# Moving the norm, split and transposes of seven graphs out of the start of a graph-attention kernel and into its steps, with 1/sqrt on GpSimd

## What is computed

```python
h = jnp.maximum(_layernorm(x, axis=-1), 0.0)
q, k, v = h @ Wq + bq, h @ Wk + bk, h @ Wv + bv          # 8 heads of 64
scores = einsum('bmhd,bnhd->bhmn', q, k) / 8 + edge_bias[edges]
scores = leaky_relu(scores, 0.2)
scores = where(edges > 0, scores, -1e9)
out = einsum('bhmn,bnhd->bmhd', softmax(scores), v) @ Wp + bp
return x + out
```

## Time and profile before

| what | us |
|---|---|
| median of 3 runs | 1028.54 (1027.62 to 1029.74) |
| the profiled execution | 1028.09 |
| its span in the profile | 1026.3 |
| PE busy | 972.7 (95%) |
| DVE busy | 885.7 (86%) |
| ACT busy | 774.3 (75%) |
| POOL busy | 489.6 (48%) |
| mean granted clock of TensorE | 0.986 |

### The profile page before, as it was taken

The page is one execution under the profiler, slowest core; times in us unless marked ns, Lnnn a source line. Parts: engine busy times, 40 slices in busy tenths (PEclk is TensorE's granted clock), DMA queues, the critical chain, the costliest instruction groups (busy, mean ns, idle before and its releaser), DMA issues. The chain is left out here.

```text
span 1026.3 us, 28211 instructions
## 1 busy us (share of the span) xinstructions
PE 972.7 (95%) x8688; PEld 941.7 (92%) x8688; DVE 885.7 (86%) x3283; ACT 774.3 (75%) x1737; POOL 489.6 (48%) x864
## 2 busy tenths in 40 slices
PE   5578999999999999999999999999999999999995
PEld 4468999999999999999999999999999999999994
DVE  4868899888998989888998899888998889988973
ACT  3577878788778887888787877787787777878852
POOL 1003445455545554555455545554554555545553
PEclk9988999999999999999999999999999999999997
DMA  7573455455555464545455455544555454544431
GB/s 175 185 246 104 128 154 141 137 136 145 138 139 146 124 168 135 144 125 159 123 150 140 134 150 144 145 133 140 150 137 144 120 151 135 162 116 130 104 75 29
DMA packets 226599, 142.21 MB, mean 139 GB/s; under 512 B 35393, under 2 KB 216141, under 8 KB 226445
## 3 DMA queue, kind: packets, MB, share of 16 engines
q1 hardware_dynamic: 225652, 139.80, 49.7%
q10 hardware_dynamic: 792, 0.53, 0.3%
HBM read 79.19 MB, written 44.04 MB: 120 GB/s over the span
## 5 line engine op out<-in xcount | busy, mean ns | idle before, releaser
L1061 POOL TENSOR_SCALAR a_line<-w,a_bias 128x256 f32<-128x256 f32 x512 | 264.8, 517 | 445.2 <-DVE w L1714 401.7
L1249 PE MATMUL bank<-pt,nat_sb 128*65 128x128 f32 x2048 | 266.0, 273 | 0.3
L1691 DVE CUSTOM_DVE_ANT_0 w<-bank,mask_rows 128x256 f32<-128x256 f32 x512 | 196.0, 420 | 78.2 <-issue 65.7
L1249 PEld LDWEIGHTS bank<-pt,nat_sb 128*65 128x65 f32 x2048 | 231.1, 138 | 0.8 <-issue 0.8
L1714 DVE SCALAR_TENSOR_TENSOR w<-w,shift,a_line 128x256 f32<-128x256 f32 x512 | 229.2, 487 | 1.7 <-POOL a_line L1061 1.5
L1474 ACT ACTIVATE pt<-bank 128x512 f32<-128x512 f32 x256 | 154.3, 603 | 101.1 <-PE bank L1202 93.4
L1703 DVE TENSOR_TENSOR onehot<-val,counts_to 128x512 fp32r<-128x512 f32 x256 | 178.1, 696 | 2.2
L1456 ACT ACTIVATE mask_own<-bank,mask_bias 128x512 bf16<-128x512 f32 x256 | 177.0, 691 | 1.1 <-PE bank L1226 1.1
L1465 ACT ACTIVATE t_sb<-bank 128x512 fp32r<-128x512 f32 x256 | 152.3, 595 | 4.0 <-PE bank L1214 3.9
L1202 PE MATMUL bank<-ident,w 128*128 128x128 f32 x1024 | 154.3, 273 | 0.0
L1191 PE MATMUL bank<-t_sb,q_hi 128*128 128x256 f32 x512 | 143.4, 302 | 3.5 <-DVE wmax L1691 3.0
(11 more groups left out here) (136 smaller groups left out, 1604.0 us busy)
## 6 DMA issues: line engine op xcount, KB each, us to landing
adj_in<-in_adj_dram SPq DMA_DIRECT2D x64, 512.0 KB, 4.0
mask_store<-mask_own SPq DMA_DIRECT2D x64, 512.0 KB, 3.5
mask_rows<-mask_store SPq DMA_DIRECT2D x512, 64.0 KB, 2.4
o_pairs<-o_turned SPq DMA_DIRECT2D x128, 128.0 KB
nl_store<-nl_ring SPq DMA_DIRECT2D x7, 512.0 KB, 4.2
stack_store<-stage SPq DMA_DIRECT2D x7, 512.0 KB, 2.9
h_stack<-stack_store SPq DMA_DIRECT2D x7, 512.0 KB, 5.5
h_nl<-nl_store SPq DMA_DIRECT2D x28, 128.0 KB, 3.8
```

The lines of the kernel that those rows point to most:

```text
L1061: nc.gpsimd.tensor_scalar(a_line[:, i % 2, :], w[:, i, :], 5.0, a_bias[:, i:i + 1], ALU.mult, ALU.add)\
L1249: last = pe.matmul(o_part[0:D + 1, P * u:P * u + P], nat_sb[:, t % 2, p % 4 * 2 + u, k, :], pt[:, p % 2, u, k, :], start=(k == 0), stop=(k ...
L1691: nc.vector.tensor_tensor_reduce(w[:, i, :], row_bank[:, SLOTS * u:SLOTS * u + SLOTS], mask_rows[:, t % 2, p % 4 * 2 + u, :], 0.25, LEAST_ ...
```

## The change

Only graph 0 is now prepared at the start. Graph g + 1 is loaded (256 KB of `x`), normed, split and turned in steps of graph g, at lags of its own: X_LOAD 8, CENTER 19, SQUARES 20, VARIANCE 21, RSTD 22, NORMED 25, HIGH 26, LOW 27, TURN_H 30 and 34. `h_nl` and `h_stack` have two slots, one for even and one for odd graphs. Stores of `h` in natural order and both loads are gone; a store of the turned `h` stays (only another branch reads it, which these inputs don't take). 1/sqrt of these graphs is made by POOL with 13 small instructions on 128 x 8 values, each waiting for the one before it (`inverse_roots`); graph 0 keeps ACT's sqrt. The transposes go through `misc`, four at a time. Beta moves from lags 6 and 10 to 10 and 14, the mean vector from 22 to 26.

The folding of the weights is cut in two. `fold_scores` has 16 products in place of 40 (bk is a 65th column of Wk, and bq is multiplied once and copied to both halves), and `fold_values` stands ahead of step 9. ACT does an Exp on one column right after the sqrt, so that its table is loaded there. The three subtractions on `kind_bias` go to the branch not taken.

```diff
-    PARTS = ((0, 8), (8, 32), (32, 64))
 
     LOAD, CONV, COUNT, TURN_A, USED, RANK, VAL, ONEHOT = 0, 4, 6, 5, 7, 8, 9, 9
-    MASK, MASK_OUT, MASK_IN, TFILL, QFILL, BETA, COLSUM, VEC = 10, 14, 15, 13, 9, 6, 18, 22
+    MASK, MASK_OUT, MASK_IN, TFILL, QFILL, BETA, COLSUM, VEC = 10, 14, 15, 13, 9, 10, 18, 26
     SCORE, A_LINE, Y, TURN, PV, X_ADD, MOVE_O, PROJ, NORM, SUM, OUT = 17, 19, 20, 21, 22, 24, 26, 31, 32, 34, 35
-    K0, SETTLED = 32, 24
+    K0 = 32
+
+    X_LOAD, CENTER, SQUARES, VARIANCE, RSTD, NORMED, HIGH, LOW, TURN_H, STORE_H = 8, 19, 20, 21, 22, 25, 26, 27, 30, 35
...
+        def coming(b, s, lag):
+
+            g = every(b, s, lag, PPG)
+            return b + g + 1 if g is not None and b + g + 1 < B else None
...
+            def load_rows(g):
+                if g >= 2:
+                    sp.wait_ge(nl_lo, g - 1)
+                sp.dma_start(rows_of(g), x_tiles[:, tiles_of(g), :]).then_inc(x_in[g % 2], 16)
...
-                g = every(b, s, LOAD, PPG)
-                if g is not None and later(b + g):
-                    if later(b + g, 2):
-                        sp.wait_ge(q_lo_ready, 32 * (b + g) - 31)
-                    load_stack(b + g)
+                g = coming(b, s, X_LOAD)
+                if g is not None:
+                    load_rows(g)
...
-                last = piece(b, s, TFILL + 1, 4)
-                if last is not None and last[0] == TPG - 1 and not (isinstance(b, int) and b == B - 1):
-                    sp.wait_ge(t_filled, 4 * TPG * b + 4 * TPG - 3 + last[1])
-                    if last[1] == 0:
-                        sp.wait_ge(col_sums, b + 1)
-                    load_natural(b + 1, last[1])
+                g = coming(b, s, STORE_H)
+                if g is not None:
+                    store_stack(g)
...
             load_rows(0)
+            load_adj(0, 0)
             sp.dma_start(bp_row, bp.rearrange("(a d) -> a d", a=1)).then_inc(wp_landed, 16)
             sp.dma_start(temp[0:1, 2896:2904], edge_bias[1:2, :]).then_inc(wp_landed, 16)
-            load_rows(1)
-            for t in range(2):
-                load_adj(0, t)
-            load_rows(2)
-            sp.dma_start(kind_bias[:, :, :].rearrange("p k h -> p (k h)"),
-                         edge_bias.rearrange("(a k) h -> a (k h)", a=1).to_broadcast([P, 5 * H])).then_inc(kinds_landed, 16)
+            load_adj(0, 1)
             for half in range(2):
                 load_x(0, half)
-            store_graph(0)
-
             for s in range(K0):
-                if s == MASK_OUT:
-                    sp.wait_ge(square_sums, B)
-                if s == SETTLED:
-                    settle(sp)
                 step(0, s)
-                k = ramp_chunk(s - 1)
-                if k is not None and k < B:
-                    store_graph(k)
...
+            def inverse_roots(g):
+
+                var, root, part = row_var[:, tiles_of(g)], row_rstd[:, tiles_of(g)], newton[:, g % 2]
+                pool.wait_ge(var_ready, g + 1)
+                nc.gpsimd.tensor_scalar(root.bitcast(I32), var.bitcast(I32), -0.5, 1597463007.0, ALU.mult, ALU.add)\
+                    .then_inc(newton_steps, 1)
+                n = 13 * (g - 1) + 1
+                for i in range(3):
+                    pool.wait_ge(newton_steps, n)
+                    nc.gpsimd.tensor_tensor(part, root, root, ALU.mult).then_inc(newton_steps, 1)
+                    pool.wait_ge(newton_steps, n + 1)
+                    nc.gpsimd.tensor_tensor(part, part, var, ALU.mult).then_inc(newton_steps, 1)
+                    pool.wait_ge(newton_steps, n + 2)
+                    nc.gpsimd.tensor_scalar(part, part, -0.5, 1.5, ALU.mult, ALU.add).then_inc(newton_steps, 1)
+                    pool.wait_ge(newton_steps, n + 3)
+                    nc.gpsimd.tensor_tensor(root, root, part, ALU.mult).then_inc(newton_steps, 1)
+                    n += 4
+                pool.wait_ge(newton_steps, n)
+                pool.nop(nofuse=True).then_inc(rstd_ready, 1)
+
             def step(b, s):
                 p = pair(b, s, A_LINE)
                 if p is not None:
                     for u in range(2):
                         line(b, p, u)
+                g = coming(b, s, RSTD)
+                if g is not None:
+                    inverse_roots(g)
...
+            def fold_scores():
+
+                for a, rows in enumerate(both):
+                    for c in range(PAIRS):
+                        pe.matmul(fold_banks[a][0:D, (D + 1) * c:(D + 1) * c + D + 1], wqT[rows, c, :], wkT[rows, c, :],
+                                  start=True, stop=True)
+                        last = pe.matmul(fold_banks[a][0:D, 264 + c:265 + c], wkT[rows, c, 0:D], bq_col[rows, c:c + 1],
+                                         start=True, stop=True)
+                last.then_inc(fold_ready, 1)
+
+            def fold_values():
+
+                pe.wait_ge(wp_landed, 16 * 3)
+                pe.wait_ge(ones_ready, 1)
+                pe.wait_ge(bias_products, PAIRS)
+                for a, rows in enumerate(both):
+                    for c in range(PAIRS):
+                        pe.matmul(value_banks[a][0:D, D * c:D * c + D], wvT[rows, c, :], wp_in[rows, c, :], start=True, stop=True)
+                    sums = value_banks[a][:, 328:332]
+                    pe.matmul(sums, ones[rows, :], bqk[rows, :], start=True, stop=False)
+                    pe.matmul(sums, ones[0:1, :], eb_row[:, a, :], start=False, stop=True)
                 for c in range(PAIRS):
-                    pe.matmul(first[0:D, D * c:D * c + D], wqT[rows, c, :], wkT[rows, c, :], start=True, stop=True)
-                    pe.matmul(first[0:D, 256 + c:257 + c], wqT[rows, c, :], bk_col[rows, c:c + 1], start=True, stop=True)
-                    pe.matmul(second[0:D, D * c:D * c + D], wvT[rows, c, :], wp_in[rows, c, :], start=True, stop=True)
-                    for dst in both:
-                        pe.matmul(second[dst, 256 + c:257 + c], wkT[rows, c, :], bq_col[rows, c:c + 1],
-                                  start=True, stop=True)
-                sums = (o_bank, misc)[a][:, 0:PAIRS]
-                pe.matmul(sums, ones[rows, :], bqk[rows, :], start=True, stop=False)
-                last = pe.matmul(sums, ones[0:1, :], eb_row[:, a, :], start=False, stop=True)
-            last.then_inc(fold_ready, 1)
-            for c in range(PAIRS):
-                pe.matmul(turn_banks[0][:, 0:D], ones, wp_bv[:, c, :], start=(c == 0), stop=False)
-            pe.matmul(turn_banks[0][:, 0:D], ones[0:1, :], bp_row, start=False, stop=True).then_inc(fold_ready, 1)
-            pe.wait_ge(folded, 6)
-
-            def turn_graph(g):
-                pe.wait_ge(nl_lo, g + 1)
-                for j in range(2 * g, 2 * g + 2):
-                    if j >= 2:
-                        pe.wait_ge(stack_copied, j - 1)
-                    for i in range(MT):
-                        last = pe.transpose(halves4[j % 2][:, P * i:P * i + P],
-                                            natural_of(g)[:, MT * (j % 2) + i, :].bitcast(F32), ident[:, :])
-                    last.then_inc(nl_turned, 1)
-
-            turn_graph(0)
-            pe.wait_ge(stack_copied, 2)
-            pe.wait_ge(consts_done, 1)
+                    pe.matmul(value_banks[0][:, 256:256 + D], ones, wp_bv[:, c, :], start=(c == 0), stop=False)
+                pe.matmul(value_banks[0][:, 256:256 + D], ones[0:1, :], bp_row, start=False, stop=True).then_inc(fold_ready, 1)
+
+            def turn_rows(g, j, dst):
+                for i in range(MT):
+                    last = pe.transpose(dst[:, P * i:P * i + P], natural_of(g)[:, MT * j + i, :].bitcast(F32), ident[:, :])
+                last.then_inc(nl_turned, 1)
...
+                        pe.wait_ge(nl_lo, g + 1)
+                        free(q_bank_uses, b, s, i)
+                        turn_rows(g, j, misc)
+                        i += 1
...
-            for s in range(K0):
+            fold_scores()
+            pe.wait_ge(plain_ready, 1)
+            for s in range(COUNT + 1):
                 step(0, s)
-                k = ramp_chunk(s)
-                if k is not None and k < B:
-                    turn_graph(k)
+            pe.wait_ge(nl_lo, 1)
+            for j in range(2):
+                turn_rows(0, j, (t_bank, m_bank)[j])
+            pe.wait_ge(consts_ready, 7)
+            for s in range(COUNT + 1, QFILL):
+                step(0, s)
+            fold_values()
+            pe.wait_ge(folded, 6)
+            pe.wait_ge(stack_copied, 2)
+            for s in range(QFILL, K0):
+                if s == SCORE:
+                    pe.wait_ge(folded, 8)
+                    pe.wait_ge(hi_weights, 10)
+                step(0, s)
...
+            def copy_turned(g, j, src):
+                act.wait_ge(nl_turned, 2 * g + j + 1)
+                if g >= 2 and j == 0:
+                    act.wait_ge(q_filled, 16 * (g - 1))
```

(68 more changed lines are left out.)

235 lines of the change are left out of this document (113 added, 122 removed).

## The result

The changed kernel takes **1038.62 us** (median of 4 runs, 1037.36 to 1039.55), the kernel before, on the same chip, 1028.08 (1026.57 to 1029.74): a ratio of 1.0101, 95% interval 1.0082 to 1.0121. It is 1.0% slower; the prediction was 1018 with a range of 1008 to 1029. The profiled execution has a span of 1036.7 us against 1026.3.

What follows compares the result with a forecast made beforehand. PE was taken to bound full load, a chain of waits the start. Span 1026.3 - 26.0 (start) + 6.1 (PE) + 1 (DVE) + 8.4 (POOL) = 1015.8, so 1018 us measured; range 1008 to 1029.

Steps and rivals of the forecast that it cites:

- The start: Before the first scores: shorter prologue and folding let DVE take them at 48.1, 26.0 us earlier, bounds 20 and 29.
- the working: Chain of waits at the start: query fill at 29.7, 16 us to scores at 45.7; weights landing 1 us sooner.
- the masks: Spread masks at the start: last copy at 38.4, then 10.7 us of store and spreading; scores taken 49.1, less 1.
- PE and DVE at full load: Each graph's added work: eight PE transposes at 0.88 us, 6.1 in seven graphs; DVE 1 us in all, bounds 0 and 4.
- POOL's term: 13 POOL instructions in step 22 delay step 24's lines; PE stalls 1.4 us, six times: 8.4 us, bounds 0 and 28.
- N: Time of POOL's 13 instructions in step 22: 3.5 us at 0.20 + 0.07 each, between 2.9 and 5.5.
- the collisions with DVE: Steps 22 and 23, POOL and DVE holding each other up: 0 to 1.4 us more, 0.2 taken.
- slack: Delay of POOL's lines before step 24 that PE's second projection does not feel: 2.2 us a graph.
- rival 3: POOL's 13 instructions cost near a 128x64 addition (5.5 us) and lose the lock; stall 4.7 us six times, 1038; chance 0.13.
- point of decision: Stall size from which POOL's roots make the kernel slower: 3.1 us (N = 5.3), giving 1028.5.

Runs made afterwards that it cites:

- the seed alone: The changed kernel with no Newton round, 1 POOL instruction in step 22 in place of 13, a root off by per cents: 1010.93 us, ratio 0.9838.
- the filled stall: The changed kernel with 22 useless PE products added in step 24, ahead of the second projection's waits: 1029.06 us, ratio 1.0025.

## Why the prediction was wrong

**The start: right in size, in part by luck.** Forecast: 26.0 us earlier, bounds 20 and 29; measured 24.6. The query fill came at 29.44 (29.7, or 28.7 with the weights 1 us sooner; they were 0.3 sooner). From there to PE's first scores it was 19.2 us and not 16: they came at 48.67, where the working has 45.7 less 1. This didn't show in the total, because the working had the masks as the last to come, at 48.1; they were there earlier, and DVE waited 0.63 us for PE.

**PE and DVE at full load: right.** Forecast 0.88 + 0.14 us a graph, so periods of 118.3; with the seed alone they are 118.3, and PE is busy 0.85 us more a period.

**POOL's term is the step that failed.** The sum has 8.4 us for the 13 instructions, six stalls of 1.4 us. They cost 4.65 us a period, 27.9 in six (122.95 with them, 118.3 with the seed alone): 19.5 us more than the sum has, which is nearly all of the miss of 20.6. It has two halves.

*The stall: the right place, the right engine, the right user, a size too small by half.* Forecast: N = 3.7, the stall N - 2.23 = 1.4 us. Measured: 4.91 and 2.99, which is 9.5 us in six. The term's parts: 13 x 0.28 = 3.6 (forecast 3.5); the collisions with DVE 1.1 (forecast 0.2); 0.24 before the heads, where the semaphore of the last instruction is waited for (0.07 in the forecast); and a slack of 1.9, not 2.2. The largest of them is the choice of 0.2 out of a range of 0 to 1.4: the argument beside it named the one-hots, and each 0.68 us one-hot that runs while small instructions stream can catch one, as two did here and two in the kernel before with the same 13. By the rule of the Trainium skill's "SBUF — State Buffer", section "SBUF: two separate sides", the prediction had the chain sit out 2.0 us. The trace agrees as to the lock: all four that were caught end 0.06 us after DVE's instruction. But each pays only what is left of that instruction when it starts: 0.44, 0.43, 0.09 and 0.12 us.

*The clock: a term that the sum has at nothing, without a reason.* It gave every microsecond of stall one microsecond. With the stall, PE's granted clock fell, and this cost 1.65 us a graph more, as the filled stall shows; 9.9 us in six. By the medians of the two kernels it is 1038.6 - 1029.1 = 9.5, or 7.5 when each is taken against the kernel before of its own group of runs. Without this fall, as the filled kernel shows, the changed one comes out 0.25% above the time before.

**The rivals.** The time of rival 3 (the roots turn the sign; 1038 us) came out, but only half of its mechanism. It wanted instructions near the cost of the 128x64 addition and a stall of 4.7 us; they cost 0.20 us each as forecast, the stall was 3.0, below its own point of decision (3.1, N = 5.3), and the clock, which it doesn't have, added the rest. That its 1038 was hit is luck. It had a chance of 0.13. With bounds of the stall up to 28 us the range would have reached 1038; it ended at 1029. "Periods differ from 119.7 by over 1 us" was named as what would prove the forecast wrong, and they did, by 3.2.
